# Storing dispatch's logits in DRAM for the combine, both stages of a soft mixture of experts in one block

## The reference

```
logits   = x @ phi                        # (256 tokens, 2048 slots)
dispatch = softmax(logits over 16 BATCHES, for each token position and slot)
combine  = softmax(logits over the 2048 slots)
slots    = dispatch.T @ x                 # (2048 slots, 128)
y        = slots of expert n @ W[n] + b[n]
out      = layernorm(x + combine @ y)     # per token
```

## Time and profile before

| | before |
|---|---|
| median of 3 runs | 1746.05 us (1741.84 to 1749.03) |
| the profiled execution: time | 1745.34 us |
| its span, first to last instruction | 1743.5 us |
| mean granted TensorE clock | 0.967 of full speed |
| PE busy | 1574.9 us (90%) |
| DVE busy | 1256.2 us (72%) |
| ACT busy | 736.6 us (42%) |
| POOL busy | 788.3 us (45%) |
| dispatch: first logits to last copy of y | 1143.25 to 1458.3 us |
| combine: first multiplication with y to last | 1482.3 to 1734.9 us |

### The profile page before, as it was taken

One profiled execution on the slowest core, in us unless ns is written; L12 is line 12 of the kernel. 1 busy time (PEld: TensorE's weight loads), 2 busy tenths in 40 slices (PEclk: granted clock), 3 DMA queues, 4 the chain that ended last, 5 costly groups with the idle time before them and its releaser, 6 DMA issues. The chain is left out here.

```text
span 1743.5 us, 36046 instructions
## 1 busy us (share of the span) xinstructions
PE 1574.9 (90%) x11520; PEld 1354.4 (78%) x11520; DVE 1256.2 (72%) x2499; ACT 736.6 (42%) x1671; POOL 788.3 (45%) x1988
## 2 busy tenths in 40 slices
PE   5489999999999999999999997359999995999998
PEld 4367777877877777777778876259999995999997
DVE  4478889879879888888988875248888882444443
ACT  2144354444534435445444431014445452555544
POOL 0333255345345445435535422237777773344443
PEclk9999999999999999999999998669999997999999
DMA  5000000000000000000000000061231324343341
GB/s 213 7 7 7 1 14 2 14 14 1 13 15 2 12 14 4 10 14 13 1 14 7 5 4 7 7 170 61 60 90 60 90 60 103 70 99 83 82 99 37
DMA packets 75942, 69.28 MB, mean 40 GB/s; under 512 B 6048, under 2 KB 69792, under 8 KB 73376
## 3 DMA queue, kind: packets, MB, share of 16 engines
q1 hardware_dynamic: 75808, 67.58, 14.6%
HBM read 44.49 MB, written 23.07 MB: 39 GB/s over the span
## 5 line engine op out<-in xcount | busy, mean ns | idle before, releaser
L631 PE MATMUL bk<-ve_f,oe 128*128 128x128 f32 x2048 | 276.8, 280 | 3.3 <-DVE ve_f L1309 3.3
L631 PEld LDWEIGHTS bk<-ve_f,oe 128*128 128x128 f32 x2048 | 248.5, 192 | 29.7 <-issue 23.9
L1309 DVE SCALAR_TENSOR_TENSOR ve_f<-ps_m,oT 128x512 f32<-128x512 f32 x256 | 173.1, 684 | 7.7 <-PE bk L631 3.3
L1953 POOL TENSOR_TENSOR d_s<-d_ex 128x1024 f32<-128x1024 f32 x32 | 129.8, 4057 | 95.1 <-ACT d_ex L1858 95.1
L1268 DVE COPY_PREDICATED vals<-oh,bk 128x512 f32<-128x512 int32 x224 | 150.5, 726 | 10.0 <-PE bk L399 9.3
L1796 PE MATMUL d_lg<-d_phf,d_xtf 128*128 (+1 forms) x1024 | 129.8, 289 | 19.7 <-DMA d_xtf<-x_T 10.3
L1796 PEld LDWEIGHTS d_lg<-d_phf,d_xtf 128*128 128x128 f32 x1024 | 126.8, 205 | 20.6 <-issue 18.4
L1807 PE MATMUL d_sl<-d_ex,d_xs 128*128 128x128 f32 x1024 | 122.2, 278 | 5.4 <-DVE d_ex L1922 5.4
L1807 PEld LDWEIGHTS d_sl<-d_ex,d_xs 128*128 128x128 f32 x1024 | 119.3, 195 | 5.7 <-DVE d_ex L1922 5.7
L397 PE MATMUL bk<-veH,x1H 128*128 128x512 f32 x256 | 116.3, 454 | 6.4 <-DVE vals L1268 6.3
L2092 PE MATMUL e_po<-e_yb,e_prT 128*128 128x128 f32 x1024 | 119.6, 275 | 0.0
(11 more groups left out here) (295 smaller groups left out, 3920.1 us busy)
## 6 DMA issues: line engine op xcount, KB each, us to landing
y_slots<-d_ys SPq DMA_DIRECT2D x64, 256.0 KB, 3.8
e_yb<-y_slots SPq DMA_DIRECT2D x64, 256.0 KB, 4.8
d_w<-W SPq DMA_DIRECT2D x16, 256.0 KB, 2.8
oe<-xT SPq DMA_DIRECT2D x1, 2048.0 KB, 8.0
xt_in<-xT SPq DMA_DIRECT2D x16, 128.0 KB, 2.2
x_in<-x SPq DMA_DIRECT2D x16, 128.0 KB, 2.3
ve_f<-v_exp SPq DMA_DIRECT2D x1, 2048.0 KB, 8.4
oe<-o_exp SPq DMA_DIRECT2D x1, 2048.0 KB, 7.6
```

Source lines behind the costliest of these rows:

```text
L631: last = pe.matmul(ps_u[:, cols], oe[:, hp, e, :], mo[:, n % MO, hp, :], start=False, stop=(e == NE - 1 and hp == HP - 1), skip_group_chec ...
L1309: V.scalar_tensor_tensor(mo[:, n % MO, :, :].rearrange("p a n -> p (a n)"), ps_m[:], float(NE - e), oT[:, u, c, :, :].rearrange("p a n -> ...
L1953: G.tensor_tensor(s8[:], e[:, 0:8, :], e[:, 8:16, :], ALU.add).then_inc(n, 1)
```

## The change

Dispatch now also keeps the logits: ACT copies each bank of a tile from PSUM to a tile `d_raw` in SBUF (`copies`), and SP stores it to a DRAM tensor `logits` of 4096 tokens x 2048 slots, in pieces of 512 B (`store_raw`). The maximum over the batches is taken in two halves of the banks, each behind ACT's copies, and a minimum of the two negated halves joins them. The combine no longer computes logits. SP loads the 1 MB of a tile's rows from DRAM (`load_l`, double-buffered by batch), DVE takes the maximum from SBUF, ACT takes the exponential in place (`weights`), and PE transposes and multiplies (`turn`, `weigh`), piece by piece in turns. The split of phi in high and low parts is gone. x3 is read from the tile that dispatch keeps. Both stages stand in one block without a barrier, with one set of PSUM banks: `tp` is `d_lg`, and `po` is two banks of `d_sl`, one for each c. The names e and q are the combine's and the dispatch's semaphores. The diff, cut to its core:

```diff
-            def logits(b, u, c):          # combine, PE: gone, with ACT's and DVE's split
-                ...
+            def copies(s, c, ks):         # dispatch, ACT
+                g = C * s + c
+                for k in ks:
+                    wait(act, q["lg_ps"], BK * g + k + 1)
+                    if k == 0:
+                        wait(act, raw_stored[c], 16 * BK * s)
+                    nc.scalar.activation(raw[:, c, k, :, :], lg[:, k, :, :], ACT.Copy).then_inc(q["raw"], 1)
+            def shifted(g, s, u, c):      # dispatch, DVE
+                wait(dve, q["sub"], 2 * g)
+                for half in range(2):
+                    wait(dve, q["raw"], BK * g + 2 * half + 2)
+                    V.tensor_reduce(mp[:, half, :],
+                                    lg[:, 2 * half:2 * half + 2, :, :].rearrange("p k b s -> p s (k b)"),
+                                    AX.X, ALU.max, negate=True).then_inc(q["max"], 1)
+                V.tensor_tensor(nm[:], mp[:, 0, :], mp[:, 1, :], ALU.min).then_inc(q["max"], 1)
+                ...
+            def store_raw(s, c):          # dispatch, SP
+                for k in range(BK):
+                    wait(sp, q["raw"], BK * (C * s + c) + k + 1)
+                    sp.dma_start(l_rows[:, k, c, :, bass.ds(s * P, P)], raw[:, c, k, :, :]
+                                 ).then_inc(raw_stored[c], 16)
+            def load_l(b, u, c):          # combine, SP
+                wait(sp, e["tp_ps"], BK * (C * (b - 2) + c + 1))
+                sp.dma_start(lt[:, u, c, :, :], l_dram[bass.ds((C * b + c) * P, P), :]
+                             .rearrange("p (s n) -> p s n", s=SB)).then_inc(l_in[u][c], 16)
+            with sp.Fori(1, NB // 2) as pair:
+                for u in range(2):
+                    for c in range(C):
+                        load_l(2 * pair + u, u, c)
+                    load_y(2 * pair + u, u)
+                    store(2 * pair + u - 2, u)
+            def turn(b, u, c, k):         # combine, PE
+                n = C * b + c
+                if k == 0:
+                    wait(pe, e["pr"], n + 1)
+                wait(pe, e["tp"], BK * (n - 1) + k + 1)
+                for j in range(4):
+                    last = pe.transpose(tp[:, k, j * P:(j + 1) * P], lt[:, u, c, 4 * k + j, :], id_f[:])
+                last.then_inc(e["tp_ps"], 1)
+            def weigh(b, u, c, k):
+                if k == 0:
+                    wait(pe, e["y"], b + 1)
+                    wait(pe, e["res"], 2 * (n - 1))
+                wait(pe, e["tp"], BK * n + k + 1)
+                ...
+            def batch(r, u, more=True):
+                for k in range(BK):
+                    turn(b, u, 1, k)
+                    weigh(b, u, 0, k)
+                for k in range(BK):
+                    if more:
+                        turn(b + 1, 1 - u, 0, k)
+                    weigh(b, u, 1, k)
+            def weights(b, u, c):         # combine, ACT
+                n = C * b + c
+                wait(act, e["max"], n + 1)
+                wait(act, e["res"], 2 * (n - 1))
+                nc.scalar.activation(part, part, ACT.Exp, bias=nmx[:, c:c + 1], accum_out=rs[:, c:c + 1]
+                                     ).then_inc(e["pr"], 1)
+            def batch(r, u, more=True):
+                turned(b, 1, (0, 1))
+                if more:
+                    weights(b + 1, 1 - u, 0)
+                turned(b, 1, (2, 3))
+                if more:
+                    turned(b + 1, 0, (0, 1))
+                    weights(b + 1, 1 - u, 1)
+                    turned(b + 1, 0, (2, 3))
+            def residual(b, u, c):        # combine, DVE
+                V.reciprocal(rr[:, c:c + 1], rs[:, c:c + 1]).then_inc(e["res"], 1)
+                wait(dve, e["out_ps"], n + 1)
+                V.scalar_tensor_tensor(rx[:, u, c, :], po[:, c, :], ...).then_inc(e["res"], 1)
+                ...
+            def batch(r, u, first=False, more=True):
+                if more:
+                    greatest(b + 1, 1 - u, 0, r + u)
+                if not first:
+                    residual(b - 1, 1 - u, 1)
+                if more:
+                    greatest(b + 1, 1 - u, 1, r + u)
+                residual(b, u, 0)
+                if not first:
+                    norm(b - 1, 1 - u, r if u else r - 1)
```

More of the change, by code:

```diff
@@ L1685, in soft_experts @@
     y_dram = nc.dram_tensor("y_slots", (SB * NS, NB * XB * D), F32, kind="Internal").ap()
-    y_stored = [kept.enter_context(nc.semaphore(f"y_stored{u}")) for u in range(2)]
-    with ExitStack() as outer:
+    l_dram = nc.dram_tensor("logits", (TT * P, S), F32, kind="Internal").ap()
+    with ExitStack() as ctx:
         def sb(name, shape, dt=F32):
[L1689 to L1700, removed]
@@ new lines, in soft_experts @@
+        loads = [sem(f"d_loads{u}") for u in range(2)]
+        raw_stored = [sem(f"d_raw_stored{c}") for c in range(C)]
+        stores = [sem(f"d_stores{u}") for u in range(2)]
+        bias_in = sem("e_bias_in")
+        l_in = [[sem(f"e_l_in{u}{c}") for c in range(C)] for u in range(2)]
+        q = {n: sem("d_" + n) for n in
+             "lg_ps raw max sub ex sum mult slot0_ps slot1_ps slot ys_ps ys".split()}
+        e = {n: sem("e_" + n) for n in "max pr tp_ps tp y out_ps res moments rstd rows".split()}
@@ new lines, in _ @@
+            with pe.Fori(1, SB // 2) as pair:
+                for u in range(2):
+                    block_of(pair, u)
+            block_of(SB // 2, 0, now=False)
+            experts(SB - 1, 1, SB // 2 - 1, 3)
+            for k in range(BK):
+                turn(0, 0, 0, k)
+            for u in range(2):
+                batch(0, u)
+            with pe.Fori(1, NB // 2 - 1) as pair:
+                for u in range(2):
+                    batch(pair, u)
+            batch(NB // 2 - 1, 0)
@@ new lines, in _, with exps, slots @@
+            batch(NB // 2 - 1, 1, more=False)
+        @block.scalar
+        def _(act):
+            def copies(s, c, ks):
+                g = C * s + c
+                for k in ks:
[3 more added lines that the diff above has]
+                    nc.scalar.activation(raw[:, c, k, :, :], lg[:, k, :, :], ACT.Copy).then_inc(q["raw"], 1)
+            def exps(s, u, c, half):
+                wait(act, q["sub"], 2 * (C * s + c) + half + 1)
+                part = ex[:, u, c, 2 * half:2 * half + 2, :, :].rearrange("p k b s -> p (k b s)")
+                nc.scalar.activation(part, part, ACT.Exp).then_inc(q["ex"], 1)
+            def slots(s, k):
+                wait(act, q["slot1_ps"], BK * s + k + 1)
@@ new lines, in _ @@
+            with act.Fori(2, SB // 2) as pair:
+                for u in range(2):
+                    block_of(pair, u)
+            block_of(SB // 2, 0, now=False)
+            weights(0, 0, 0)
+            slots(SB - 1, 3)
+            outputs(SB - 1, 1, SB // 2 - 1, 2)
+            outputs(SB - 1, 1, SB // 2 - 1, 3)
+            weights(0, 0, 1)
+            turned(0, 0, range(BK))
+            for u in range(2):
+                batch(0, u)
+            with act.Fori(1, NB // 2 - 1) as pair:
+                for u in range(2):
+                    batch(pair, u)
```

762 lines of the change are left out of this document (328 added, 434 removed).

## The result

The changed kernel takes **1807.41 us** (median of 4, 1801.90 to 1813.31), the kernel before 1745.67 us on the same chip: ratio 1.036, 95% interval 1.032 to 1.039, so it is 3.6% slower. The forecast was 1798, range 1740 to 1840. The profiled execution took 1801.9 us with a span of 1800.1; 1797.5 had been worked out for it.

What follows compares the result with a forecast made beforehand. PE was taken to bound dispatch and combine, the changed combine its new waits. First product at 1472.9, plus 314.2 of combine, 8.6 of tail and 1.84 outside the span: 1797.5 us, 1798 beside the median; range 1740 to 1840.

Steps and rivals of the forecast that it cites:

- Both waits: Combine: PE waits 2.7 us a tile for residual and exponential; every second tile DVE's maximum waits for logits queued behind SP's store.
- Start: Dispatch's beginning: first logits go bank by bank behind quarter loads, without the split of phi; -5 us (0 to -7).
- Dispatch's block: Dispatch: a block of slots takes 18.1 us instead of 17.87, +3 us over 13 blocks.
- Handover: Between dispatch and combine: no barrier and no logits first, but weights ahead of the last slot copies; -5.8 us (+-4).
- Batch: Combine, two tiles: 18.0 us at full clock plus 2.5 for the lower clock, 20.5 us; range 19 to 22.5.
- The load: Combine: 1 MB of a tile's logits from DRAM takes 4.8 us, with bounds of 3.1 and 7.6.
- Tail: End of the combine: norm and store behind the last product take 8.6 us, as before.
- (1): Rival, combine: PE's clock stays up behind its gaps; 1762 us, chance 0.14.
- (2): Rival, combine: clock stays up and loads land within 3.2 us, only the exponential is waited for; 1741 us, chance 0.09.
- (3): Rival, combine: exponentials are ahead and PE bounds, 10.7 us a batch; 1653 us, chance 0.06.
- (4): Rival, dispatch: stores of logits in 512 B pieces bound it, a block 24 us; near 1890 us, chance 0.09.
- the list: Expected signs in the profile: combine's PE busy about 55%, granted clock near 0.8, two kinds of gap, dispatch blocks 18.1 us.

Runs made afterwards that it cites:

- e1: Changed kernel with ACT's exponential waiting for the reciprocal of tile n-2 instead of that tile's residual: 1795.2 us.
- e2: Changed kernel with only SP's order in the combine changed, loads of logits issued as soon as their buffer is free, ahead of the store: 1793.2 us.
- e3: Changed kernel with the edits of e1 and e2 together: 1710.3 us.
- e6b: Changed kernel with dispatch's two half reductions and their minimum put back into one reduction over four banks: 1814.0 us.
- e6: Changed kernel with dispatch's minimum of the two halves made a reduction over one operand: 1808.7 us.
- e5: Changed kernel with PE's gaps in the combine filled by 20 or 32 unread transposes behind each tile's products: 1796.4 us.
- e11: e9 with the residual's result moved to an unused PSUM bank: 1656.9 us.
- e8: Changed kernel with loads ahead of stores, two buffers for the exponentials' sums, and y read in 8 KB pieces, stored in 512 B ones: 1681.5 us.
- e9: e8 with y's load issued ahead of the load of the next batch's first logits: 1690.2 us.

## Why the prediction was right

**The mechanism held.** Both waits are there in the places named, with the engines named, and each covers the other (e1, e2, e3). The combine's length is 313.9 us against 314.2 forecast and 252.6 before; that the two agree within 0.3 is luck, since the same combine took up to 319.4 (e6b). The 61.3 us over the kernel before are more than the whole loss of the profiled executions (56.6), since the first product starts 4.8 earlier. Step by step:

- Start: first logits at 1139.28 instead of 1143.25, third block's at 1178.00 instead of about 1186.6. 8.6 us gained, 5 forecast. Since the first logits of thirteen profiles with this same beginning lie between 1133 and 1144, 4 of the 8.6 are no more than that; from the first logits to the third block it is 38.7 against 43.4 us. These 4.7 are near the 5 of the forecast, but it had looked for them ahead of the first logits.
- Dispatch's block: 18.58 us in the rows above, forecast 18.1. Mis-sized, +0.5 a block; the thirteen from 1178.00 to 1420.62 took 242.6 us where 235.3 were forecast. Of the 0.5 a block, 0.3 is the chain (7.70 for 7.4), of which 0.2 is the minimum's length beside POOL (e6); the other 0.2 is PE's own stretch (10.88 for 10.7), which e6 did not shorten.
- Handover, from the start of the last logits to the first product: 49.2 us, where 54.5 - 5.8 = 48.7 were forecast.
- First product at 1477.51 for 1472.9: -3.6 from the start, +7.3 from the thirteen blocks, and under 1 from the last tile and the handover.
- Batch: 20.4 us, forecast 20.5, but by two errors that cancel. From the end of (b,0)'s products to the residual of (b,1) it is 10.7 us (1606.79 to 1617.51), forecast 9.9: the load is issued 1.23 us behind the store's start, not 0.56. The rows named for the 0.56 do not give it, and the trace of before has 1.24 at that place, the store at 1582.12 and the load behind it:

```profile
1583.36 0.35 SPq L2028 DMA_DIRECT2D e_xtf<-x_T  x1
```

  From that residual to the end of the next products it is 9.7 us (to 1627.23), forecast 8.1 + 2.5 = 10.6: the clock costs 1.6 there and not 2.5. The gap of 2.85 us costs 1.6 too. As the forecast had it, that lies beside the wait for the load; but the longer first tile shortens the second gap, 3.3 us instead of 4.3, and the forecast had left that out. Whether the smaller cost comes of the shorter gap isn't shown: behind 7.6 us it was 2.0 (e1).
- The load: 4.9 us for 1 MB, taken 4.8. The Trainium skill (DMA: Bandwidth & Descriptors, the two cost components) makes it an estimate of 4.4; the trace lies above it.
- Tail 8.7 us, forecast 8.6.

**The rivals.** (1), the clock stays up: refuted by the rows at 1609.63 and by e5. (2), quick loads: 4.9 us and DVE waits for them 13 times. (3), PE bounds: wrong for this kernel, right for the one without its waits; e11 has its 10.64 us a batch. (4), stores of logits bound dispatch: PE waits there 0.2 to 0.3 us a block and for DVE; 183 GB/s were moved at a share of 0.65, which makes some 280 at a full share (an estimate from that row). The 215 of the earlier trace rows, read in one microsecond, had priced these pieces too high; it changed nothing in the sum, which had put the stores at nothing. With y's stores in 512 B pieces as well the block didn't change (e8).

**What the list had said.** PE "about 55%" busy was 70%, since a tile at the lower clock counts as busy; the granted clock was 0.83 for 0.8.

## What to carry to other kernels

Work taken from the bound engine pays only as far as the other engines' order lets it: before counting a saving, follow what the freed engine waits for next, all the way round the loop, the queue that issues its loads included. Where two waits stand in one loop, taking either away shows almost nothing (12 and 14 us here) and both together 97; an experiment that moves little is no proof that its wait is harmless. An instruction of an engine off the path can be stretched by its neighbour: look at an operation's duration in the new place, not only at its place.

## What the hardware showed that was not expected

- DVE and POOL hold each other up by what DVE reads. A 128x128 minimum of two SBUF operands took 0.63 to 1.40 us beside POOL's additions and ended with them, as a reduction over one operand 0.43. A 128x128 norm took 2.4 us on the mean beside POOL's 4.5 us bias (e9) and 0.41 with its source in PSUM (e11). DVE's maxima over one operand (2.29 us) never changed. The other way round, POOL's 128x1024 addition, 2.35 us at its shortest, took 3.60 us when it began 0.9 us into DVE's division of two SBUF operands (1300.55). The Trainium skill (SBUF — State Buffer, "SBUF: two separate sides") says that a DVE operation with two SBUF inputs, or one in a mode that uses two ports, and an operation of POOL that reads SBUF take a shared pair of ports for their whole length, and the later one waits. These rows agree; that the norm is of the second kind is an inference from them. The prediction had left this out when it gave the minimum 0.3 us.
- A gap of 2.71 us before PE's work cost nothing at 1488.22 and 1.6 us of clock at 1496.47, one tile on; in the loop 2.85 us cost 1.6. In e5 1.98 us cost as much, and one of 7.6 us (e1) made the following tile 7.6 us long, 2.0 above full clock. Two gaps of the same length fall on different sides, so the length of a gap alone doesn't tell what it costs.
- 512 B stores of 2.1 MB a block ran beside everything else in dispatch without a wait on PE, while the same piece size in the combine, at 245 GB/s and a share of 0.9, was worth 23 us.
